# GNN kernel, graph build: each window's edges in five tiles of 64 + 64 edges in place of six tiles of 128, with paired 64-row key matmuls

## The reference, cut

```python
edge_index = jnp.stack([src, dst])
h = jnp.maximum(_layernorm(x), 0.0);  x = x + L0(h, src, dst)                 # degree-normalised sum
h = jnp.maximum(_layernorm(x), 0.0);  x = x + L1(h, edge_index, ...)          # two attention layers
h = jnp.maximum(_layernorm(x), 0.0);  x = x + L2(h, edge_index, ...)          # one attention layer, rows normalised
h = jnp.maximum(_layernorm(x), 0.0);  x = x + L3(h, edge_index, edge_weight1) # two linear message layers, log_softmax
# L0: agg = segment_sum((h * out_deg**-0.5)[src], dst) * in_deg**-0.5
# L3: msg = cat[x[dst], x[src], edge_attr] @ W + b; agg = segment_sum(msg, dst)
```

## Time and profile before

| | us |
|---|---|
| median of 3 runs (lowest, highest) | 2967.22 (2966.0, 2977.09) |
| the profiled execution, its own time | 2972.84 |
| its span in the trace | 2971.0 |
| of it, the build: first to last key matmul | 227.8 to 1023.7 |

### The profile page before, as it was taken

One profiled execution on the slowest core, in us unless ns is written; L12 is line 12 of the kernel. 1 busy time (PEld: TensorE's weight loads), 2 busy tenths in 40 slices (PEclk: granted clock), 3 DMA queues, 4 the chain that ended last, 5 costly groups with the idle time before them and its releaser, 6 DMA issues. The chain is left out here.

```text
span 2971.0 us, 77270 instructions
## 1 busy us (share of the span) xinstructions
PE 2569.7 (86%) x26152; PEld 2159.6 (73%) x26153; DVE 2307.2 (78%) x5557; ACT 1604.4 (54%) x2016; POOL 355.0 (12%) x866
## 2 busy tenths in 40 slices
PE   3648999999999959999787888759999967999998
PEld 2645666666666649999666777649999957888997
DVE  8979999999999966676699999979999995222212
ACT  6023444444444349999797888658888841000101
POOL 0003344434444300000000000000000000000000
PEclk8878999999999979999999999879999978999999
DMA  3003443343344436667345545315545616888898
GB/s 102 0 1 83 119 121 82 100 134 88 94 118 110 134 109 218 231 224 256 134 153 174 193 157 191 130 66 175 195 161 186 215 65 241 306 301 300 314 368 297
DMA packets 448144, 493.83 MB, mean 166 GB/s; under 512 B 132101, under 2 KB 447465, under 8 KB 447850
## 3 DMA queue, kind: packets, MB, share of 16 engines
q1 hardware_dynamic: 300920, 409.16, 41.2%
q10 hardware_dynamic: 147060, 82.71, 9.5%
HBM read 402.61 MB, written 89.17 MB: 166 GB/s over the span
## 5 line engine op out<-in xcount | busy, mean ns | idle before, releaser
L2594 PE MATMUL psum<-sb_arena 128*128 128x198 bf16 (+2 forms) x14406 | 1118.1, 238 | 148.0 <-DVE sb_arena L1881 86.5
L2594 PEld LDWEIGHTS psum<-sb_arena 128*128 128x128 f16 x14406 | 1045.0, 99 | 220.8 <-DVE sb_arena L1881 139.6
L3211 ACT ACTIVATE sb_arena<-sb_arena 128x896 f16 (+1 forms) x1029 | 1016.4, 1046 | 157.6 <-PE psum L2594 122.2
L1875 DVE TENSOR_TENSOR sb_arena<-sb_arena 128x896 f16<-128x896 f16 x1029 | 634.9, 621 | 139.4 <-ACT sb_arena L3211 117.9
L1166 DVE TENSOR_SCALAR sb_arena<-sb_arena 128x392 f16<-128x392 f16 x2352 | 582.1, 312 | 0.0
L2873 ACT ACTIVATE sb_arena<-psum 128x784 f16<-128x784 f32 x392 | 323.3, 825 | 440.4 <-PE psum L2240 388.8
L2240 PE MATMUL psum<-sb_arena 128*128 128x392 f16 x2352 | 483.6, 343 | 39.7 <-ACT sb_arena L2835 22.2
L2659 PE MATMUL psum<-sb_arena 128*128 128x192 bf16 x4802 | 412.1, 247 | 27.2 <-DVEq L2006 15.7
L2659 PEld LDWEIGHTS psum<-sb_arena 128*128 128x128 f16 x4802 | 401.4, 98 | 36.7 <-DVEq L2006 16.4
L1881 DVE TENSOR_TENSOR sb_arena<-sb_arena 128x896 f16<-128x896 f16 x686 | 423.0, 617 | 0.0
L2240 PEld LDWEIGHTS psum<-sb_arena 128*128 128x128 bf16 x2352 | 290.6, 128 | 165.9 <-issue 63.8
(11 more groups left out here) (378 smaller groups left out, 1267.6 us busy)
## 6 DMA issues: line engine op xcount, KB each, us to landing
sb_arena<-counts SPq DMA_DIRECT2D x245, 896.0 KB, 6.6
sb_arena<-counts SPq DMA_DIRECT2D x245, 672.0 KB, 4.6
counts<-sb_arena ACTq DMA_DIRECT2D x56, 1344.0 KB, 5.6
sb_arena<-records SPq DMA_DIRECT2D x392, 6.0 KB, 1.7
sb_arena<-records ACTq DMA_DIRECT2D x392, 6.0 KB, 1.7
counts<-sb_arena SPq DMA_DIRECT2D x1, 5488.0 KB, 19.6
records<-sb_arena SPq DMA_DIRECT2D x1, 3124.0 KB, 8.9
counts<-sb_arena ACTq DMA_DIRECT2D x14, 112.0 KB, 1.7
```

Of the source, the lines that this page charges most:

```text
L1875: nc.vector.tensor_tensor(above_at[r % RING], above_at[r % RING], counts_of(g, j), ALU.mult).then_inc(above_ready, 1)
L2594: last = nc.tensor.matmul(psum[:, bank, at:at + wide], of[:, b * BLK:(b + 1) * BLK], moves[side][:, r, :], start=(r == 0 and at == 0), sto ...
L3211: nc.scalar.activation(above_at[r % RING], of, ACT.Sigmoid, bias=steep_s[:, r:r + 1], scale=STEEP).then_inc(signs_ready, 1)
```

## The change

A window's two groups are now held side by side: partitions 0 to 63 carry edges of one group, 64 to 127 those of another. Five tiles (`ST = 5`) hold 320 edges of each group (`CAP = ST * SIDE`), in place of three tiles of 128 for each. The two groups of a window are no longer neighbours: `group_of` takes group k of a set of eight for the lower half and group k + 4 for the upper. What follows from it:

- DVE: `sub_src` is made for two windows at once (128 x 1280, 196 instructions in place of 392 of 128 x 768), and `sub_key` in five instructions per window in place of six. DVE waits once per pair of windows. `ea_hit` has 160 columns in place of 192. Four pairs of small instructions at the start set `ea_own`, in place of one.
- PE: ten key matmuls per window in place of six. Each has 64 rows (the edges of one half of the partitions), 128 weight columns and 392 data columns; the two of a pair use the same tile number and go to two PSUM banks.
- PE: `edge_sum` has ten fp32 matmuls in place of three, each with 64 rows, 32 weight columns and 4 data columns, into two banks (4 and 5). Its wait on `ea_ready` now stands ahead of the last pair of sums.
- SP and ACT load 64-partition records (5 x 16 bytes each) in place of 128-partition ones (3 x 16 bytes). POOL handles 15 values per partition in place of 18.
- ACT writes the counts of a window to `stage` in the new order of groups; the copy has the same size. `LEA` is kept per side, and the two sides are masked and added at the end of the build.

The sums behind, `chunk_back`, and everything after the build are as before.

```diff
-ST = 3
-CAP = ST * BLK
+ST = 5
+SIDE = BLK // 2
+CAP = ST * SIDE
...
+        def group_of(k, side):
+            return k // EG * 2 * EG + side * EG + k % EG
...
                 with dve.Fori(0, NH) as h:
                     for k in range(WH):
-                        s, at = k % WS, k % SS
-                        dve.wait_ge(rel_ready, h * WH + (k + WS + 1))
-                        dve.wait_ge(window_done, h * WH + (k + 1))
-                        nc.vector.tensor_tensor(sub_src[:, at], iota_t[:, :, 0:2 * ST],
-                                                src_rel[:, s, :].unsqueeze(1).broadcast_to([BLK, BLK, 2 * ST]), ALU.is_equal)
-                        for t in range(2 * ST):
-                            last = nc.vector.tensor_scalar(sub_key[:, at, t, :], sub_iota[:, t // ST, :],
-                                                           rel[:, k, 3 * t:3 * t + 1], None, ALU.is_equal)
+                        at = k % SS
+                        if k % 2 == 0:
+                            dve.wait_ge(rel_ready, h * WH + (k + WS + 2))
+                            dve.wait_ge(window_done, h * WH + (k + 2))
+                            nc.vector.tensor_tensor(sub_src[:, at // 2], iota_t[:, :, 0:2 * ST],
+                                                    src_rel[:, k:k + 2, :].rearrange("p w t -> p (w t)").unsqueeze(1).broadcast_to([BLK, BLK, 2 * ST]), ALU.is_equal)
+                        for t in range(ST):
+                            last = nc.vector.tensor_scalar(sub_key[:, at, t, :], sub_iota[:], rel[:, k, 3 * t:3 * t + 1], None, ALU.is_equal)
...
                 def edge_sum(odd, i, h):
-                    p0, at = g % 2 * EG * WIN, g // 2 * 2 * EG
-                    wins = rel[:, i * EG:(i + 1) * EG, :].rearrange("p w (g t c) -> p (w g) t c", t=ST, c=3)
-                    pe.wait_ge(ea_ready, h * (WH // EG) + (i + 2))
+                    at = g // 2 * EG
                     for t in range(ST):
-                        last = nc.tensor.matmul(psum[p0:p0 + EG * WIN, 5, at:at + 2 * EG], ea_hit[:, i % HITS, t * EG * WIN:(t + 1) * EG * WIN], wins[:, :, t, 2],
-                                                start=t == 0, stop=t == ST - 1, skip_group_check=True)
+                        for side in range(2):
+                            rows, p0 = slice(side * SIDE, (side + 1) * SIDE), (g % 2 * 2 + side) * EG * SUB
+                            last = nc.tensor.matmul(psum[p0:p0 + EG * SUB, 4 + side, at:at + EG], ea_hit[rows, i % HITS, t * EG * SUB:(t + 1) * EG * SUB],
+                                                    rel[rows, i * EG:(i + 1) * EG, 3 * t + 2], start=t == 0, stop=t == ST - 1, skip_group_check=True)
...
-                            for t in range(2 * ST):
-                                last = nc.tensor.matmul(psum[:, k % 2 * 2 + t // ST, 0:NB * SUB], sub_src[:, s, :, t],
-                                                        sub_key[:, s, t, :], start=t % ST == 0, stop=t % ST == ST - 1)
+                            for t in range(ST):
+                                for side in range(2):
+                                    rows = slice(side * SIDE, (side + 1) * SIDE)
+                                    last = nc.tensor.matmul(psum[:, k % 2 * 2 + side, 0:NB * SUB], sub_src[rows, s // 2, :, k % 2 * ST + t],
+                                                            sub_key[rows, s, t, :], start=t == 0, stop=t == ST - 1)
```

More of the change, by code:

```diff
@@ L671, in _ @@
             with sp.If(fast == 1):
-                with sp.Fori(0, NWIN // WS) as i:
-                    for s in range(WS):
-                        sp.wait_ge(rel_ready, i * WS + s + 1)
-                        packed = sp.value_load(starts[0:1, bass.ds(i * 2 * WS + 2 * s, 1)], min_val=0, max_val=(TILES * BLK - CAP) * PACK)
-                        sp.dma_start(rec[:, s, 0, :], records[bass.ds(packed // PACK, CAP), :].rearrange("(p t) c -> p (t c)", p=BLK)).then_inc(rec_in[s], 16)
+                with sp.Fori(0, NH) as h:
+                    for k in range(WH):
+                        sp.wait_ge(rel_ready, h * WH + (k + 1))
+                        packed = sp.value_load(starts[0:1, bass.ds(h * 2 * WH + group_of(k, 0), 1)], min_val=0, max_val=(TILES * BLK - CAP) * PACK)
+                        sp.dma_start(rec[0:SIDE, k % WS, :], records[bass.ds(packed // PACK, CAP), :].rearrange("(p t) c -> p (t c)", p=SIDE)).then_inc(rec_in[k % WS], 16)
                 sp.wait_ge(stage_ready, NH + 1)
@@ L2186, in _ @@
                     last = nc.tensor.matmul(psum[:, 6 + b, 0:HALF], zero_b[:, 0:BLK], iota_t[:, 0:HALF // HT, :], start=True, stop=True)
-                nc.tensor.matmul(psum[:, 5, 0:CB * 2 * EG], zero_b[:, 0:BLK], zero_b[:, 0:CB * 2 * EG], start=True, stop=True)
+                for b in range(2):
+                    last = nc.tensor.matmul(psum[:, 4 + b, 0:CB * EG], zero_b[:, 0:BLK], zero_b[:, 0:CB * EG], start=True, stop=True)
                 last.then_inc(half_summed, 1)
```

99 lines of the change are left out of this document (59 added, 40 removed).

## The result

The changed kernel takes 2988.82 us in the median of 10 runs (2980.63 to 2997.54), the kernel before 2973.69 us beside it (10 runs, 2965.98 to 2983.38). The ratio is 1.0043 (95%: 1.0025 to 1.006): 15 us slower, under half a per cent. The forecast was 3055 us with 3005 as its lower end. The direction was right; the size was too large, +88 us forecast and +15 measured. By the prediction's own mark (0.5%, 15 us) the result counts as no difference, a case to which it had given 0.07; the interval of the ratio still leaves out 1.

The account below looks back on a forecast made before the run. PE's own work was taken to bound the build. Four windows cost 4 x 0.14 + 0.44 = +1.0 us, a half +6.5, 14 halves +91, with the ends +92, rounded down to +88: 3055 us, range 3005 to 3155.

Parts of the forecast that it names:

- What bounds the kernel: Build: PE's own work sets a half's time, with DVE 5% behind it.
- DVE's price: DVE in the build: `sub_src` plus ten `sub_key` take 3.06 us for two windows in place of 3.72.
- The matmuls: PE's ten key matmuls: the two of a pair run together, 0.85 us against 1.02 for six before.
- Rivals 1 and 2: Key matmul pairs: run one after the other, 3375 us (chance 0.06); or weight loads hold them up, 3147 us (chance 0.08).
- The change of shape: PE, between 64-row keys and 128-row sums: array emptied twice per window, 2 x 0.14 = 0.28 us.
- The edge sum: PE's twenty fp32 matmuls: 0.90 us, 1.02 with the shape change, against 0.58 before; +0.44 us for four windows.
- ACT with slack: Build: ACT's copy takes 0.82 us in a window of 1.9, so ACT keeps its slack.
- The +0.5 for each turn: First four windows of a half: +0.5 us, with part of the cost hidden in the wait for ACT.
- Rival 3: Turns of a half: gaps at shape changes lengthen the half-clock stretch, +48 us, 3103 to 3141; chance 0.08.
- Rival 4: PE's shape changes: no emptying between 128 and 64 rows, 2921 to 2943 or about 2963 us; chance 0.14.
- my case: Whole kernel: pairs overlap but shape changes and edge sum cost more; 3055 us, bounds 3016 to 3093, chance 0.64.

Follow-up runs that it names:

- two-by-two run: Changed kernel with the key matmuls of two windows in a row, then the sums of both; 2973.42 us, 1.0009 of the kernel before.
- the run with the edge sum's sides apart: Changed kernel with an edge sum's 20 matmuls ordered as one side's ten, then the other's; 3000.51 us, 1.0102 of the kernel before.
- the stores by SP: Changed kernel with PE's chunk loop written out, two windows' keys in a row, and SP issuing each half's five stores instead of ACT; 2927.29 us, 0.9845 of before.
- the loop written out: Changed kernel with PE's loop over the seven chunks written out, so no jump back is left; 2986.62 us, 1.0054 of the kernel before.
- both: Changed kernel with PE's chunk loop written out and the key matmuls of two windows in a row; 2971.19 us, 0.9986 of the kernel before.

## Why the prediction was wrong

**What bounds the kernel: right.** PE sets a half, DVE does not: it took 94 us more of work and the build did not get longer. DVE's price was right too: the trace has 703.43 to 706.48, 3.05 us for two windows, where I had 3.06.

```profile
703.43 0.81 DVE L1181 TENSOR_TENSOR sb_arena<-sb_arena 128x1280 bf16<-128x1280 bf16 x1
704.17 2.39 DVE L1184 TENSOR_SCALAR sb_arena<-sb_arena 128x392 f16<-128x392 f16 x10
706.48 0.32 DVE L1190 TENSOR_TENSOR sb_arena<-sb_arena 128x160 f32<-128x160 f32 x1
```

**The matmuls: right.** Pairs run together, five streams of 0.166. The Trainium skill's rule that different tiles load and multiply in parallel (TensorEngine Tiling (Array Packing), Key Properties) holds here, with 4 to 7 ns between the two of a pair. Rivals 1 and 2 fell with it.

**The change of shape: mechanism right, size a little high.** Emptying is 0.09 us both times: the last sum's columns end at 703.74 + 0.19 = 703.93, the next load begins at 704.02. With the loads in sight I measure about 0.15 on the way into the pairs (0.10, and 0.05 more between the first pair and the second, 0.217 for 0.166) and 0.10 on the way out, 0.25 in all, and the two-by-two run gave 0.25 for the same. I had 0.28 and 0.03 more for the second load. A window came to 1.84 - 1.77 = +0.07 in place of +0.14.

**The edge sum: this step failed.** In the prediction's sum it is the +0.44 us for four windows. I took 0.90 us for twenty matmuls, "between" 0.64 and 1.28, and the true value, 0.31, is below my lower bound. I got that bound by halving the 0.064 of a start before for the overlap of the sides alone. Two savings multiply here and I allowed one. A group by itself starts every 0.032 us: so do the first group's matmuls of the run with the edge sum's sides apart (708.087 to .246), before the second group begins at 708.251. And two groups overlap, so a pair costs 0.032 and one matmul 0.016. Which of the half rows, half weight columns and half data makes the 0.032, no run separates. The fourth window costs 2.25 - 1.84 = 0.41 us more than another, where it was 0.58. So the edge term is -0.17 and not +0.44 for four windows, the wrong sign, and over the 84 groups of four windows in the forecast 51 us of the 73 between +88 and +15. The window's +0.07 in place of +0.14 is another 24.

**The sum.** 4 x 0.07 - 0.17 = +0.11 us for four windows (7.77 against 7.66), where I had +1.0. Windows 4 to 26 of a half (23 windows with five edge sums) give 23 x 0.07 - 5 x 0.17 = +0.8 us, 43.6 in place of 42.8 where nothing disturbs them, 14 x 0.8 = 11 us. Another 5 us are in halves of 44.1 to 45.0, and 3.8 of them in one place: window 20 of the halves 0, 2, 4, 6, 8 and 10, where ACT has just issued the half's last store; that issue takes 1.10 to 1.55 us in these six halves and 0.44 or 0.45 in the odd ones up to half 11. PE waited 4.1 us for ACT's copies of windows, the wait that the stores by SP later took away; the forecast had ACT with slack. The +0.5 for each turn did not come. That makes the 16 us. So the right direction is in part luck: the windows' two terms alone come to 11 us, and a wait that was not forecast brings the rest.

**The jump: a term that was missing and that cost nothing.** The forecast counts the matmuls that the change adds and not what it means for the loop to hold them (1419 instructions in a pass become 2259). The cost of 20.6 us was covered by a wait that stood behind it. That it would have cost 35 us (1.2%) without that cover is this sum, and no run shows it.

**Rival 3** fell: 65.6 us of the build at half clock against 74.0 before. **Rival 4** had put the dividing price at 0.07 per change of shape; the changes cost 0.10 and 0.15. The time fell between my case and this rival because the edge sum got cheaper, which the rival named (0.64 to 0.90) but also sized too high. The range was too narrow at the fast end: its end came from a sum in which every step had its lowest value, and one lowest value was itself an assumption. The case's upper end has a slip, too: 6 x 1.38 + 0.5 in 14 halves, with the 1 us and the 4 us, is +120 and 3087, not +126 and 3093.

## What to carry to other kernels

When a matmul is split by rows, price the passage from one shape to the other (here 0.25 us there and back) against the streams it saves, and put as much work of one shape in a row as the buffers allow. When several savings fall on one small instruction (narrower, shorter, in parallel), let each have its own factor in the lower bound. Look up what an engine waits for next before counting a wait as lost or a saved wait as won: here six jumps of 3.6 us cost nothing, and 5 store issues a half cost nothing until PE had become faster, and then were worth 27 us in the windows.

## What the runs showed of the hardware

- **The jump back of a long loop body waits.** It took 0.21 us with 1419 and with 1699 instructions in the body, and 3.6 to 4.7 us with 2259; PE's instruction queue then carried 144 packets in place of 75, which I read as the body being fetched again in every pass. Inside the body nothing waits for it: at equal windows the pitch is the same with the loop written out (1.84).
- **Row groups do not wait for each other in program order.** The sixth key matmul of the program began 0.226 us after the first, ahead of the third. The Trainium skill says that matmuls start and end strictly in program order (TensorE: Matmul & The Clock Gate, The mechanism); between two row groups the starts above contradict it, within one group they agree.
- **Small fp32 matmuls**: 64 x 32 weights and 4 data columns start every 0.032 us in one row group, and with two groups at once every 0.016. With 128 x 64 and 8 columns the six of the earlier trace rows start 0.058 apart behind a first step of 0.080, 0.31 us in all, as long as the twenty take after.
- **An increment of a semaphore on PE's queue** takes 0.150 us of the queue; five in a row behind six key matmuls (0.75 us) were hidden, fifteen (some 2.3 us in a window that took 1.8) were not.
- **The spread of runs goes with the clock.** Over the 75 runs of the kernel before that stand beside the experiments, the mean granted clock lay between 0.930 and 0.939 and the time followed it by some 20 us per 0.01. At the same mean clock (0.935, by a line fitted over all the runs of these kernels) the changed kernel is at 2991, the written-out loop at 2987, the keys two by two at 2973, both at 2970, and the stores by SP at 2938. The order of the medians stays, and part of the last one's gain (10 us) is a higher clock, 0.939 in the mean, that this kernel was granted in its runs.
